# Edge scores of a graph attention kernel: another split of the source number, and one maximum in place of product and sum

## The reference, cut to what matters

```python
xp = (x @ W).reshape(N, H, C)                      # N = 3125 nodes, H = 4 heads, C = 256
a_src = einsum('nhc,hc->nh', xp, att_src)          # 4 numbers per node
a_dst = einsum('nhc,hc->nh', xp, att_dst)          # 4 numbers per node
e = leaky_relu(a_src[src] + a_dst[dst], 0.2)       # 50000 edges, sorted by dst, and the self loops
m = segment_max(e, dst); ee = exp(e - m[dst]); alpha = ee / segment_sum(ee, dst)[dst]
x = x + relu(segment_sum(xp[src] * alpha) + bias)  # x is layer-normed before the product with W
x = x + ffn(layernorm(x))                          # 8 experts, the best two per node
```

## Time and profile before

| | |
|---|---|
| median of 3 runs | 2160.12 us (2158.95 to 2163.76) |
| span of the profiled execution (the only time given for it) | 2296.1 us |
| PE busy | 1959.2 us, 85% |
| VectorE busy | 1470.6 us, 64% |
| ScalarE busy | 1137.3 us, 50% |
| GpSimd busy | 768.2 us, 33% |
| stage 1 | up to 332.0 us |
| stage 2, from the first group's matmul to the last sum | 332.7 to 482.7 us |

### The profile page before, as it was taken

The page is one execution under the profiler, slowest core; times in us unless marked ns, Lnnn a source line. Parts: engine busy times, 40 slices in busy tenths (PEclk is TensorE's granted clock), DMA queues, the critical chain, the costliest instruction groups (busy, mean ns, idle before and its releaser), DMA issues. The chain is left out here.

```text
span 2296.1 us, 53233 instructions
## 1 busy us (share of the span) xinstructions
PE 1959.2 (85%) x14846; PEld 1318.7 (57%) x14847; DVE 1470.6 (64%) x4341; ACT 1137.3 (50%) x2499; POOL 768.2 (33%) x943
## 2 busy tenths in 40 slices
PE   6999977667878888888888589983899999999997
PEld 4666545645766667777667455652454445555553
DVE  7988859987666666666666699867543443443333
ACT  4444421113666666676666566654543443443332
POOL 1020000022555555555555232321233333333332
PEclk9999976568999999999999889995899999999999
DMA  7444544403988888888888677746646556644542
GB/s 272 134 143 136 172 131 172 186 0 114 312 281 291 286 299 287 294 296 287 287 298 294 235 249 240 228 142 234 233 169 249 212 167 239 221 160 171 176 162 80
DMA packets 135664, 490.15 MB, mean 213 GB/s; under 512 B 16900, under 2 KB 17108, under 8 KB 133410
## 3 DMA queue, kind: packets, MB, share of 16 engines
q0 software_dynamic: 95568, 334.62, 43.5%
q1 hardware_dynamic: 31954, 125.15, 15.1%
q10 hardware_dynamic: 8064, 29.36, 3.7%
HBM read 419.17 MB, written 81.17 MB: 218 GB/s over the span
## 5 line engine op out<-in xcount | busy, mean ns | idle before, releaser
L1130 PE MATMUL main_ps<-rows,O 128*128 128x256 f16 x4992 | 619.2, 283 | 125.7 <-DVE acc L1066 66.3
L1113 ACT ACTIVATE O<-O,pk 128x128 f16<-128x128 f16 x1664 | 502.9, 387 | 246.1 <-DVE O L1083 203.5
L1130 PEld LDWEIGHTS main_ps<-rows,O 128*128 128x128 f16 x4992 | 480.9, 102 | 217.9 <-issue 72.8
L1052 POOL DMA_INDIRECT rows<-projected,idx x416 | 395.5, 951 | 325.2 <-PE small_ps L1135 202.9
L1087 DVE TENSOR_SCALAR O<-O,pk 128x128 f16<-128x128 f16 x1664 | 314.6, 273 | 15.0 <-issue 0.2
L1837 PE MATMUL x_h<-w_p,gram 128*128 x1344 | 307.1, 386 | 18.4 <-ACT gram L1787 7.6
L1852 PE MATMUL x_o<-w_p,gram 128*128 x1344 | 308.0, 379 | 1.4 <-ACT gram L1806 1.4
L1886 PE MATMUL pj_ps<-gram,xsT 128*125 128x512 f16 x1200 | 271.1, 385 | 8.8 <-ACT xsT L402 5.5
L1837 PEld LDWEIGHTS x_h<-w_p,gram 128*128 128x128 f16 x1344 | 131.6, 99 | 171.6 <-issue 31.5
L1886 PEld LDWEIGHTS pj_ps<-gram,xsT 128*125 128x125 f16 x1200 | 163.2, 139 | 104.7 <-ACT xsT L402 8.6
L1083 DVE TENSOR_SCALAR O<-iota,pk 128x128 f16<-128x128 f16 x416 | 109.4, 263 | 164.9 <-PE small_ps L1135 124.1
(11 more groups left out here) (346 smaller groups left out, 2538.9 us busy)
## 6 DMA issues: line engine op xcount, KB each, us to landing
w_f<-in_L_ffn_W_dram SPq DMA_DIRECT2D x14, 2048.0 KB
b_t<-in_L_ffn_b_dram ACTq DMA_DIRECT2D x56, 512.0 KB
projected_f<-xp_f POOLq DMA_DIRECT2D x25, 500.0 KB, 3.7
projected<-xp POOLq DMA_DIRECT2D x25, 500.0 KB, 4.6
out_dram<-n_x SPq DMA_DIRECT2D x25, 500.0 KB
x_after_gnn_normed<-PK POOLq DMA_DIRECT2D x25, 500.0 KB, 9.1
xt<-in_x_dram SPq DMA_DIRECT2D x24, 512.0 KB, 3.3
n_own<-projected_f SPq DMA_DIRECT2D x24, 512.0 KB, 13.0
```

The source lines that it names most:

```text
L1052: pool.indirect_dma_start(out=rows[:, 4 * p + k, :, :].rearrange("k n d -> k (n d)"), out_offset=None, in_=xp_d[:, :], in_offset=bass.Indi ...
L1113: ins = act.activation(O[:, k, 1 + HEADS + h, :], O[:, k, 0, :], ACT.Copy, scale=pk[:, p, k, w:w + 1])
L1130: pe.matmul(main_ps[:, h * C:(h + 1) * C], O[:, k, 1 + HEADS * a + h, :], rows[:, 4 * p + k, b, h * C:(h + 1) * C], start=first and h % 2 ...
```

## The change

A source is split by `LOW` = 116 in place of 125: `src = 116 a + r`, with `a` from 0 to 26 (`HI` is now 27). The upper number `a` is itself split into two digits, `a = 9 t + u`, with t from 0 to 2 and u from 0 to 8. The stationary operand's 128 rows are now: 116 one-hot rows for `r`, 3 for `t`, 9 for `u`. They come from three arrays in DRAM in place of one (`lo_d`, `third_d`, `unit_d`), each broadcast to its own partitions (`parts_of`); with the local destination that makes four loads per chunk in place of two. The table (`terms`) has 27 x 4 columns for each part; in its first 116 rows stand the node terms, moved there from `st16` by small matmuls with a shifted identity, and in its last 12 rows a mask: 0 where the digit of the row fits the column, -65504 elsewhere. So in PSUM the one column of the right `a` holds the score, and all others hold it with a large negative number added; the product and the sum become one maximum that reads PSUM. `hi_oh`, `high_one_hots`, `pick` and `total` are gone. PE now waits for `s_got`, the maximum of group n-2.

```diff
+        def parts_of(lo, dl):
+            end = LOW + HI // TENS
+            return (lo[0:LOW], lo_d), (lo[LOW:end], third_d), (lo[end:P], unit_d), (dl, dloc_d)
...
+                            sp.dma_start(third_d.rearrange("(p r) n -> p (r n)", r=4), rowV[:, 2, :]).then_inc(s_vstore, 16)
+                            sp.dma_start(unit_d.rearrange("(p r) n -> p (r n)", r=4), rowV[:, 3, :]).then_inc(s_vstore, 16)
-                    sp.wait_ge(s_vstore, 32)
-                    sp.wait_ge(s_tr_ix, 3)
-                    for t, d in ((stage_lo, lo_d), (stage_dl, dloc_d)):
-                        sp.dma_start(t, d[0:CHUNK, :].partition_broadcast(P)).then_inc(s_row[0], 16)
+                    sp.wait_ge(s_vstore, 64)
+                    sp.wait_ge(s_tr_ix, 2)
+                    for t, d in parts_of(stage_lo, stage_dl):
+                        sp.dma_start(t, d[0:CHUNK, :].partition_broadcast(t.shape[0])).then_inc(s_row[0], 16)
...  (edge_numbers, at block 13)
-                        dve.scalar_tensor_tensor(fV[:, 2, :], fV[:, 1, :], -float(ROWS), fV[:, 0, :], ALU.mult, ALU.add)
+                        dve.scalar_tensor_tensor(rowV[:, 0, :], fV[:, 1, :], -float(LOW), fV[:, 0, :], ALU.mult, ALU.add)
+                        link(dve.tensor_scalar(fV[:, 2, :], fV[:, 1, :], 1.0 / TENS, -0.5 * (TENS - 1) / TENS, ALU.mult, ALU.add))
+                        link(dve.tensor_scalar(fV[:, 2, :], fV[:, 2, :], WHOLE, None, ALU.add))
+                        link(dve.tensor_scalar(fV[:, 2, :], fV[:, 2, :], -WHOLE, None, ALU.add))
+                        dve.tensor_copy(rowV[:, 2, :], fV[:, 2, :])
+                        dve.scalar_tensor_tensor(rowV[:, 3, :], fV[:, 2, :], -float(TENS), fV[:, 1, :], ALU.mult, ALU.add)
...
-                        dve.tensor_copy(rowV, fV[:, 2:4, :]).then_inc(s_rowv, 1)
+                        dve.tensor_copy(rowV[:, 1, :], fV[:, 3, :]).then_inc(s_rowv, 1)
...  (VectorE's loop over the blocks; the turn of the third array goes, digit_mask is 18 small operations)
-                        if i in (15, 17, 19):
+                        if i in (15, 17):
                             turned_numbers((i - 15) // 2)
+                        if i == 16:
+                            digit_mask()
-                        if 17 <= i < 25:
-                            high_one_hots(i - 17)
...  (VectorE at the end of stage 1)
+                    dve.wait_ge(s_spread, 1)
+                    dve.tensor_copy(terms[:, :, :, :], spread_ps)
...  (PE at the end of stage 1)
+                    pe.matmul(spread_ps, ident16[:, :], mask[:, :, :, :], start=True, stop=True, skip_group_check=True)
+                    for n, blocks in enumerate((range(LATE), range(LATE, BLOCKS))):
+                        pe.wait_ge(s_st16, 2 * n + 2)
+                        for b in blocks:
+                            for a in range(ROWS * b // LOW, (ROWS * (b + 1) - 1) // LOW + 1):
+                                w = P - (ROWS * b - LOW * a)
+                                ins = pe.matmul(spread_ps[0:LOW, :, a, :], shift16[0:ROWS, w:w + LOW], ...)
+                    ins.then_inc(s_spread, 1)
...  (stage 2: SP, VectorE, PE)
-                        for t, d in ((lo_b, lo_d), (dl_b, dloc_d)):
-                            sp.dma_start(t[p], d[CHUNK * i:CHUNK * (i + 1), :].partition_broadcast(P)).then_inc(s_row[p], 16)
+                        for t, d in parts_of(lo_b[p], dl_b[p]):
+                            sp.dma_start(t, d[CHUNK * i:CHUNK * (i + 1), :].partition_broadcast(t.shape[0])).then_inc(s_row[p], 16)
...
-                        dve.wait_ge(s_row[p], 32 * (j + 1))
-                        dve.tensor_scalar(lo_b[p], lo_b[p], iota_col[:, 0:1], None, ALU.is_equal)
+                        dve.wait_ge(s_row[p], 64 * (j + 1))
+                        dve.tensor_scalar(lo_b[p], lo_b[p], src_row[:, 0:1], None, ALU.is_equal)
...
-                            dve.tensor_tensor(pick[:, b, :, :, :], s_ps[b][:, :, :].rearrange("k v (a h) -> k v h a", h=HEADS),
-                                              hi_oh[:, four(n), :].unsqueeze(2).broadcast_to([P, 4, HEADS, HI]), ALU.mult).then_inc(s_sel, 1)
-                            if not early(n, 1):
-                                total(n - 1, 1 - b)
+                            dve.tensor_reduce(sT[:, four, :], s_ps[b][:, :, :].rearrange("k v (a h) -> k v h a", h=HEADS), AX.X, ALU.max).then_inc(s_got, 1)
...
-                                pe.wait_ge(s_sel, n - 1)
+                                pe.wait_ge(s_got, n - 1)
...
-                                    pe.matmul(s_ps[(p + q) % 2][:, u, :].rearrange("k (a h) -> k a h", h=HEADS), lo_b[p][0:ROWS, 4 * q + u, :],
-                                              st16[:, :, h0:h0 + HEADS], start=(part == 0), stop=(part == 1))
+                                    pe.matmul(s_ps[(p + q) % 2][:, u, :], lo_b[p][:, 4 * q + u, :],
+                                              terms[:, part, :, :].rearrange("r a h -> r (a h)"), start=(part == 0), stop=(part == 1))
```

More of the change, by code:

```diff
@@ L51 @@
 CHUNK = VISITS // 8
-HI = -(-NODES // P)
+LOW, TENS = 116, 9
+HI = -(-NODES // LOW)
+DIGITS = HI // TENS + TENS
+MASK = -65504.0
 WS = 64.0
@@ L226, in program @@
         early_ctx = ExitStack()
-        hiT = sbuf(early_ctx, "hiT", [P, VISITS], F16)
-        hi_oh = PK[:, :, :].rearrange("k v n -> k (v n)").bitcast(U8)[:, 0:VISITS * HI].rearrange("k (v a) -> k v a", a=HI)
+        src_row = sbuf(early_ctx, "src_row", [P, 1])
+        terms = sbuf(early_ctx, "src_terms", [P, 2, HI, HEADS], F16)
         dstV = sbuf(early_ctx, "dstV", [VP, ROW4])
@@ L254, in program @@
             fV = cut(VP, 8 * ROW4, 4 * ROW4, None).rearrange("v (n a) -> v n a", n=4)
-            rowV = cut(VP, 12 * ROW4, ROW4, F16).rearrange("v (n a) -> v n a", n=2)
+            rowV = cut(VP, 6 * ROW4, 2 * ROW4, F16).rearrange("v (n a) -> v n a", n=4)
+            shift16 = sbuf(c, "shift16", [P, 3 * P], F16)
+            digit = sbuf(c, "digit", [P, 4])
+            digits_of = sbuf(c, "digits_of", [P, 3, HI])
+            mask = sbuf(c, "mask", [P, 2, HI, HEADS], F16)
+            s_spread = sem("ed_spread")
             cnt = sbuf(c, "cnt", [98, BLOCKS - 1])
@@ L591, in term_parts, with digit_mask @@
                         dve.tensor_tensor(st16[:, bs, 2 * HEADS:], stN[:, bs, :], st16[:, bs, 0:2 * HEADS], ALU.subtract).then_inc(s_st16, 1)
[L593 to L599, removed]
+                    def digit_mask():
+                        top = HI // TENS
+                        dve.memset(shift16[:, 0:P], 0.0)
+                        dve.memset(shift16[:, 2 * P:], 0.0)
+                        dve.tensor_copy(shift16[:, P:2 * P], ident)
+                        link(dve.tensor_scalar(digit[:, 0:1], iota_col[:, :], LOW - 0.5, -float(LOW), ALU.is_gt, ALU.mult))
+                        link(dve.tensor_scalar(digit[:, 1:2], iota_col[:, :], LOW + top - 0.5, -float(top), ALU.is_gt, ALU.mult))
+                        link(dve.tensor_tensor(digit[:, 2:3], digit[:, 0:1], digit[:, 1:2], ALU.add))
+                        link(dve.tensor_tensor(src_row[:, :], iota_col[:, :], digit[:, 2:3], ALU.add))
+                        link(dve.tensor_scalar(digits_of[:, 0, :], iota_row[:, 0:HI], 1.0 / TENS, -0.5 * (TENS - 1) / TENS, ALU.mult, ALU.add))
+                        link(dve.tensor_scalar(digits_of[:, 0, :], digits_of[:, 0, :], WHOLE, None, ALU.add))
+                        link(dve.tensor_scalar(digits_of[:, 0, :], digits_of[:, 0, :], -WHOLE, None, ALU.add))
+                        link(dve.scalar_tensor_tensor(digits_of[:, 1, :], digits_of[:, 0, :], -float(TENS), iota_row[:, 0:HI], ALU.mult, ALU.add))
+                        dve.tensor_scalar(digit[:, 3:4], iota_col[:, :], LOW - 0.5, MASK, ALU.is_gt, ALU.mult)
+                        link(dve.tensor_scalar(digit[:, 1:2], iota_col[:, :], LOW + top - 0.5, None, ALU.is_gt))
+                        link(dve.tensor_tensor(digits_of[:, 1, :], digits_of[:, 1, :], digits_of[:, 0, :], ALU.subtract))
+                        link(dve.scalar_tensor_tensor(digits_of[:, 2, :], digits_of[:, 1, :], digit[:, 1:2], digits_of[:, 0, :], ALU.mult, ALU.add))
+                        link(dve.tensor_scalar(digits_of[:, 0, :], digits_of[:, 2, :], src_row[:, :], digit[:, 3:4], ALU.not_equal, ALU.mult))
+                        for part in range(2):
+                            dve.tensor_copy(mask[:, part, :, :], digits_of[:, 0, :].unsqueeze(2).broadcast_to([P, HI, HEADS]))
@@ L712, in _ @@
                             ins.then_inc(s_wordT, 1)
[L713 removed]
+                        if i in (13, 15):
                             turn_numbers((i - 13) // 2)
+                    pe.wait_ge(s_trc, 2)
+                    pe.matmul(spread_ps, ident16[:, :], mask[:, :, :, :], start=True, stop=True, skip_group_check=True)
[4 more added lines that the diff above has]
+                                w = P - (ROWS * b - LOW * a)
```

(4 more changed lines are left out.)

30 lines of the change are left out of this document (11 added, 19 removed).

## The result

The changed kernel takes 2273.71 us (median of 4, 2270.79 to 2276.00) against 2159.67 of the kernel before (4 runs): the ratio is 1.0519, 95% interval 1.0499 to 1.0540, so 5.2% or 114 us slower. The forecast was slower, but by 75 us: the time lies outside the stated range, 2216 to 2258. The path was the one forecast; one term of its sum, the time of the busiest DMA engine's rows, was 4.9 us too small for each chunk.

A forecast was written before the change was run, and what follows sets the result against it. VectorE was taken to bound stage 2, thinly, with data ready 0.5 us before use. Forecast: 2160.1 + 64.8 (stage 2) + 10.0 (stage 1) = 2234.9 us, range 2216 to 2258.

The forecast's parts named there:

- What bounds the kernel now: Stage 2: VectorE bounds a chunk at 17.8 us, but thinly, as data is there 0.5 us before use.
- The number of engines: Chunk loads: a load uses the largest divisor of its rows up to 16, so 116 rows get 4 DMA engines.
- Length of a row: Chunk loads: 13,312 bytes take 0.50 us; 39 rows on the busiest engine 19.5 us, issue to use 22.0.
- rival D: Chunk loads: rows of 0.65 us on the few engines, 27 us from issue to use, 2273 us; chance 0.04.
- The rest of the ring: Stage 2, a chunk's period of 28.5 us: besides the loads' 22.0, build 3.7 and tail 2.8.
- tail: Stage 2, from a build's end to the next issue of loads: 2.8 us, was 2.7.
- The last run: Stage 2, from the last build's start to the last maximum: 22.3 us in place of 24.2, so -1.9.
- Stage 2: Later first build, five longer periods, later last build and a shorter end: +64.8 us in all.
- the row term: Chunk loads: the busiest engine's 39 rows at 0.50 us each, 19.5 us.
- Stage 1: Blocks without high_one_hots faster, small operations added, build_first's data 11.5 us later: +10.0 us in all.
- Hidden work: End of stage 1: spreading the terms by small matmuls is covered by GpSimd's end, cover over 6 us.
- Profile against median: Differences read from the 2296.1 us span were put unchanged on the 2160.1 median; doubt 5 us.

The follow-up runs named there:

- 120 + 8: The kernel before, with its load of lo to 128 partitions cut into one of 120 and one of 8: 2199.1 us, ratio 1.0174.
- 64 + 64: The kernel before, with its load of lo to 128 partitions cut into two of 64: 2186.9 us, ratio 1.0128.

## Why the prediction was right in kind and too small

**What bounds the kernel now: right.** The data of a chunk was ready only just before its use: that the bound of VectorE was thin is what two runs show together: half of VectorE's work with the data 12.6 to 13.8 us after its issue gives nothing (2163.2), and the same with earlier loads gives 2152.7.

**The number of engines: right.** The largest divisor up to 16 gives 4 for 116, share 0.25. It was read from 125, 104 and 128 rows, and 116, 120, 112 and 64 in the experiments fit it. The semaphore increments that the traces record from DMAs fit too: 35 for a chunk's loads in the changed kernel, 41 with 120 + 8 and 48 with 64 + 64. That is 4 + 3 + 9 + 16, 15 + 8 + 16 and 16 + 16 + 16, if each load on fewer than 16 engines makes one more; the one more is read from these counts.

**Length of a row, the step that failed.** The term was "at 26.6 GB/s 0.50 us", for all 39 rows of the busiest engine, 19.5 us, and 22.0 from issue to use. Measured from issue to use: 26.3 to 27.2, 26.9 in the middle. The last 15 us run at 0.50 a row; in the first 10 us rows take 1.0. 7 loads x 4.9 = +34 us in stage 2. I took the rate from transfers over 128 partitions and from 125 rows that ran alone, and put the engines' number as the only thing that differs. In the changed kernel the load of 128 runs beside that of 116, and while it does both write at half rate; by itself each ran at full rate (414 GB/s, and 106 on 4 engines). With 120 and with 64 + 64 the halving is there with all 16 engines busy. So the time of a row hangs on which partitions are written at one time; why in the changed kernel all 16 engines are slowed, and not only some, stays open. The case of slower rows was in the text as rival D, 0.65 us and 2273; its time is nearly the measured one, its picture (all rows slower) is not, and it had 0.04.

**The rest of the ring: right.** Build 3.7, tail 2.8 forecast and 2.79 measured, maximum 0.6 and 0.61, period 33.4 = 26.9 + 3.7 + 2.8. The last run, from the last build (572.9) to 593.9, is 21.0, forecast 22.3. **Stage 2:** +64.8 forecast, +98.3 measured; the difference is 33.5, the row term's +34 with -1.3 of the last run and less than 1 us elsewhere.

**Stage 1:** +10.0 forecast, +13.0 measured. Without high_one_hots a block takes 11.25 us (252.64 to 263.89), as forecast. digit_mask costs block 16 1.5 us (12.77), less than the 2.0 counted; the loads go out at 266.3 in place of 268.8, -2.5 where I had -1.5. build_first starts 30.6 us after them, forecast 26.1: the same term once more, +4.5.

**Hidden work: right.** The spread table is there at 337.86 (VectorE's copy), and GpSimd's end lasts from 337.9 to 344.8, so it costs nothing.

**Profile against median.** I let the difference stand for both, with 5 us of doubt, for a spread of 136 us that came from one disturbed stage. That was harmless here, since the gather isn't touched; a profile whose span stands far from the runs should be taken again before anything is read from it.

## What to carry to other kernels

When a slice of partitions changes its size, work out the load anew: how many DMA engines the new row count gives, and which partitions they write at one time; 128 partitions as one load were the best of all that ran here, and rows that need other data can be loaded over them afterwards, which made the data 1.7 to 2.9 us later here. Before halving an engine's work, look how long before its use the next thing is there; here that was 0.5 us, and only earlier loads made the halved work count. A rate read from transfers of one shape, or running alone, is an end of a range for another shape and not its middle.

## What was not expected of the hardware

While a load over 64 neighbouring partitions runs, or one over 120, the engines move 240 and 224 GB/s, with one over 112 311, where with one over 128 they move 414 to 429. The share of busy engines (1.03 to 1.07 in the slow stretches, 1.00 and 1.01 in the fast ones) doesn't show it; the GB/s beside it does.
